# Splitting the attention weights and building the 4-bit weights in pieces beside the MLP units

## What is computed

```python
x = x + layernorm(mamba_mixer_and_mlp(layernorm(x)))      # L0_attn: mixer, then a gated MLP of width 1792
x = x + layernorm(lora_mlp(layernorm(x)))                 # L0_ffn: gated MLP of width 1376, LoRA of rank 16
x = x + layernorm(attention(layernorm(x)))                # L1_attn: 32 heads of 16, 8 kv heads, causal, RoPE
x = x + layernorm(lut_linear(layernorm(x)))               # L1_ffn, below
# lut_linear, with e = norm of a token's row:
w_l = dequant_kbit(qweight, lut4, 4)    # (512, 512): each weight is one of 16 values of its row
w_h = dequant_kbit(qweight, lut8, 8)    # the same from 256 values
y = where(e > 64, x @ w_h.T, x @ w_l.T) + bias
```

## Time and profile before

| | us |
|---|---|
| median of 3 runs | 1904.93 (1902.29 to 1907.94) |
| the profiled execution | 1906.81 |
| its span, first to last instruction | 1905.0 |
| TensorE busy | 1666.1 (87%) |
| VectorE busy | 1037.7 (54%) |
| ScalarE busy | 793.0 (42%) |
| GpSimd busy | 601.3 (32%) |

### The profile page before, as it was taken

The page is one execution under the profiler, slowest core; times in us unless marked ns, Lnnn a source line. Parts: engine busy times, 40 slices in busy tenths (PEclk is TensorE's granted clock), DMA queues, the critical chain, the costliest instruction groups (busy, mean ns, idle before and its releaser), DMA issues. The chain is left out here.

```text
span 1905.0 us, 25873 instructions
## 1 busy us (share of the span) xinstructions
PE 1666.1 (87%) x8965; PEld 1393.2 (73%) x8965; DVE 1037.7 (54%) x2013; ACT 793.0 (42%) x1603; POOL 601.3 (32%) x792
## 2 busy tenths in 40 slices
PE   5999986999999999999999998028889889899884
PEld 4899874888888888778778887026778778777763
DVE  7888755522232226753433234755767767767772
ACT  4676643222122112212212111406867776776760
POOL 5454551211111113431111134124344444444422
PEclk9999997999999999999999999558999999999996
DMA  4000002000011012310110001200000000000000
GB/s 134 13 23 12 1 1 78 23 23 21 25 34 31 23 35 75 103 59 15 34 37 27 21 23 44 76 1 1 1 1 12 12 1 12 12 1 13 12 7 18
DMA packets 28548, 52.16 MB, mean 27 GB/s; under 512 B 3520, under 2 KB 4704, under 8 KB 28416
## 3 DMA queue, kind: packets, MB, share of 16 engines
q1 hardware_dynamic: 28416, 50.47, 8.5%
HBM read 42.07 MB, written 8.39 MB: 26 GB/s over the span
## 5 line engine op out<-in xcount | busy, mean ns | idle before, releaser
L1171 POOL TENSOR_TENSOR m_a_lo<-m_prod,m_a_hi 128x512 fp32r<-128x512 f32 x100 | 130.8, 1308 | 640.3 <-ACT m_a_hi L1229 640.2
L1345 DVE TENSOR_TENSOR m_prod<-m_prod,m_ps 128x512 f32<-128x512 f32 x100 | 68.8, 688 | 482.0 <-ACT m_prod L1225 481.9
L114 PE MATMUL m_ps<-m_hT_hi,m_w_hi 128*128 128x512 f32 x800 | 317.8, 397 | 7.5 <-DVE m_w_lo L1327 5.3
L116 PE MATMUL m_ps<-m_hT_hi,m_w_lo 128*128 128x512 f32 x800 | 317.7, 397 | 0.0
L115 PE MATMUL m_ps<-m_hT_lo,m_w_hi 128*128 128x512 f32 x800 | 317.1, 396 | 0.0
L1225 ACT ACTIVATE m_prod<-m_ps 128x512 f32<-128x512 f32 x100 | 59.7, 597 | 577.9 <-PE m_ps L116 577.9
L1802 ACT ACTIVATE t_p<-t_ps,t_nmax 128x128 f32<-128x128 f32 (+1 forms) x512 | 181.0, 424 | 75.0 <-DVE t_nmax L1924 74.8
L1924 DVE TENSOR_REDUCE t_nmax<-t_ps 128x2 f32<-128x512 f32 (+1 forms) x192 | 132.0, 688 | 96.6 <-PE t_ps L1993 60.1
L114 PEld LDWEIGHTS m_ps<-m_hT_hi,m_w_hi 128*128 128x128 f32 x800 | 151.3, 189 | 44.1 <-issue 5.7
L115 PEld LDWEIGHTS m_ps<-m_hT_lo,m_w_hi 128*128 128x128 f32 x800 | 151.2, 189 | 36.3
L116 PEld LDWEIGHTS m_ps<-m_hT_hi,m_w_lo 128*128 128x128 f32 x800 | 151.0, 189 | 36.4
(11 more groups left out here) (259 smaller groups left out, 3732.4 us busy)
## 6 DMA issues: line engine op xcount, KB each, us to landing
m_raw<-in_w_mlp SPq DMA_DIRECT2D x75, 256.0 KB, 2.7
a_xt<-in_x SPq DMA_DIRECT2D x8, 512.0 KB, 3.8
m_old<-in_x SPq DMA_DIRECT2D x16, 256.0 KB, 4.2
x_store<-stream SPq DMA_DIRECT2D x4, 1024.0 KB, 5.1
m_old<-x_store SPq DMA_DIRECT2D x16, 256.0 KB, 2.7
out<-t_yl SPq DMA_DIRECT2D x16, 256.0 KB, 2.0
q_raw<-in_w_attn SPq DMA_DIRECT2D x10, 256.0 KB, 5.1
a_att<-in_w_mixer SPq DMA_DIRECT2D x8, 256.0 KB, 2.8
```

The lines of the kernel that those rows point to most:

```text
L114: pe.matmul(out, w_hi, x_hi, start=first, stop=False)
L116: return pe.matmul(out, w_lo, x_hi, start=False, stop=last)
L1171: pool.tensor_tensor(a_lo[:, n % 2, :], prod[:, :], f(a_hi[:, n % 2, :]), ALU.subtract).then_inc(lo, 1)
L1345: dve.tensor_tensor(prod[:, :], prod[:, :], ps[:, U + TURN_AT["unit", n, 0] % 2, :], ALU.mult).then_inc(prodd, 1)
```

## The change

`split_weights` and `lut_weights_by_tree` are gone. Their work is done inside `mlps`, and attention follows directly.

- The tree is cut into 16 pieces of 128 columns (`TREE_COLS`), one for every two spots of groups 1, 2 and 3 (`TREE_AT`). At the first of the two ScalarE fills eight leaves and VectorE makes four masks; at the second VectorE does the 15 predicated copies. Leaves lie in `m_tok` and planes, tables and masks in `m_old`, which those groups don't use. SyncE stores each piece to a DRAM buffer `w4_store` (`store_tree`).
- In the last group ten pieces "attn" load and split the attention weights into the weight set that is free then, and four pieces "lut" load the 4-bit weights back, turn them on TensorE and split them. The table `LATE` says which at which spot.
- Buffers are shared so that this fits: block 0's `hT` lies in the LUT weights, `ln2` in `bias`, the mixer's `hT` too in the LUT weights.
- In attention GpSimd clears `v` and `kT` behind the first two `roots("x", ...)`; those who read them wait for it themselves.
- `JOBS_AT` is another table, and with it some steps of VectorE and GpSimd are at other slots.

```diff
+TREE_COLS, TREE_BITS = 128, 4
+TREE_LEAVES = 2 ** TREE_BITS // 2
+TREE_PIECES = DT * DIM // TREE_COLS
+TREE_SPOTS = [(g, i, j) for g in (1, 2, 3) for i in range(NB) for j in range(GROUPS[g][1])]
+TREE_AT = {TREE_SPOTS[2 * r + part]: (r, part) for r in range(TREE_PIECES) for part in range(2)}
+LATE = ((("attn", 0), ("attn", 1)), (("attn", 2), ("attn", 3)), (("attn", 4), ("attn", 5)), (("lut", 0),), (("attn", 6),),
+        (("lut", 1),), (("attn", 7),), (("lut", 2),), (("attn", 8), ("attn", 9)), (("lut", 3),))
...
+            def tree_leaves(r):
+                act.wait_ge(tree_in, 48)
+                if r:
+                    act.wait_ge(picks, TREE_PICKS * r)
+                else:
+                    act.wait_ge(tp, TPB * NB)
+                for n in (*range(1, TREE_LEAVES), 0):
+                    if n == 0 and r:
+                        act.wait_ge(tree_out, 16 * r)
+                    act.activation(leaf(n), entry(r, 2 * n), ACT.Copy).then_inc(leaves, 1)
...
+            def store_tree(r):
+                sp.wait_ge(picks, TREE_PICKS * (r + 1))
+                sp.dma_start(w4_store[:, r * TREE_COLS:(r + 1) * TREE_COLS], leaf(0)).then_inc(tree_out, 16)
...
+            def tree_picks(r):
+                dve.wait_ge(masks, TREE_BITS * (r + 1))
+                dve.wait_ge(leaves, TREE_LEAVES * (r + 1))
+                for n in range(TREE_LEAVES):
+                    dve.copy_predicated(leaf(n), mask(0), entry(r, 2 * n + 1)).then_inc(picks, 1)
...
+                    for n in range(0, TREE_LEAVES, 2 * step):
+                        dve.copy_predicated(leaf(n), mask(p), leaf(n + step)).then_inc(picks, 1)
...
+            def lut_turned(q):
+                pe.wait_ge(raw_in[q % RAW], 16 * (q // RAW + 1))
+                k = turn_free(("lut", q, 0))
+                for a in range(DT):
+                    mm = pe.transpose(ps[:, G + k, a * P:(a + 1) * P], raw[:, q % RAW, a * P:(a + 1) * P], ident)
...
 JOBS_AT = (
-    (("k", 1, 1, 0), ("q", 3, 0, 0)),
+    (("q", 3, 0, 0),),
...
+    (("x", 0, 1, 1), ("k", 1, 1, 0)),
     (("kv", 0, 0, 1),),
-    (("x", 0, 1, 1),),
...
-    (("back", 1, 0, 0), ("l", 0, 0, -1)),
-    (("l", 1, 0, -1), ("q", 2, 1, 1)),
-    (("back", 1, 1, 0), ("h", 0, 1, -1)),
+    (("back", 1, 0, 0), ("h", 0, 1, -1)),
+    (("q", 2, 1, 1), ("l", 0, 0, -1)),
+    (("back", 1, 1, 0), ("l", 1, 0, -1)),
...
-                if n == 6 and in_batch(b + 1):
+                if n == 7 and in_batch(b + 1):
                     rope_sum(0, b + 1)
...
-                if n in (0, 5) and in_batch(b + 1):
-                    normalise("x", n // 5, b + 1)
+                if n in (0, 4) and in_batch(b + 1):
+                    normalise("x", n // 4, b + 1)
...
-                if n in (17, 20) and in_batch(b - 1):
-                    normalise("h", n // 20, b - 1)
+                if n in (17, 18) and in_batch(b - 1):
+                    normalise("h", n - 17, b - 1)
```

More of the change, by code:

```diff
@@ L116, in product @@
     return pe.matmul(out, w_lo, x_hi, start=False, stop=last)
[L119 to L152, removed]
 PAIRS, CONVS = 5, 3
@@ L997, in weight_pieces @@
             pieces.append(piece)
+    spots = [(NG - 1, i, j) for i in range(NB) for j in range(GROUPS[NG - 1][1])]
+    for spot, beside in zip(spots, LATE):
+        for what, k in beside:
+            of_weight[what, k, 0] = len(pieces)
+            ready.setdefault(spot, []).append(len(pieces))
+            pieces.append((what, k, 0))
     return pieces, of_weight, ready
@@ L1026, with mlps @@
 LORAS = [q for q, piece in enumerate(PIECES) if piece[0] == "lora"]
-def mlps(nc, d, consts, stream, x1_store):
+LUTS = [q for q, piece in enumerate(PIECES) if piece[0] == "lut"]
+def mlps(nc, d, consts, stream, x1_store, w4_store, lut, bias, late, late_2):
     with ExitStack() as ctx:
         m = Memory(nc, ctx)
-        sets = [[m.sb(f"m_w{s}_{p}", [P, 3 * UNIT], F32R) for p in ("hi", "lo")] for s in range(2)]
+        late_cols = late.rearrange("p k n -> p (k n)")
+        sets = [[m.sb(f"m_w0_{p}", [P, 3 * UNIT], F32R)[:, :] for p in ("hi", "lo")],
+                [late_cols[:, 0:3 * UNIT], late_cols[:, 3 * UNIT:6 * UNIT]]]
         RAW = 3
@@ L1046, in mlps @@
         f_rs, e_rs = (m.sb(f"m_{n}_rs", [P, 4, TPB]) for n in "fe")
-        hT_hi = m.sb("m_hT_hi", [P, DT, TOK], F32R)
-        hT_lo = m.sb("m_hT_lo", [P, DT, TOK], F32R)
+        hT_hi, hT_lo = ([own] + [m.sb(f"m_hT{i}_{p}", [P, DT, BT], F32R) for i in range(1, NB)] for own, p in zip(lut, ("hi", "lo")))
         ps = m.banks("m_ps")
@@ L1063, in mlps @@
         stored, const = sem("stored"), sem("const")
+        tree_in, leaves, masks, picks, tree_out, lut_tp, bias_in = (
+            sem(n) for n in ("tree_in", "leaves", "masks", "picks", "tree_out", "lut_tp", "bias_in"))
         x_in, x1_out = (ap.rearrange("(t p) n -> p t n", p=P) for ap in (d["x"], x1_store))
@@ L1083, in units_to, with leaf, mask, entry @@
             return NB * GROUPS[g][0]
+        def leaf(n):
+            return tok[:, n // 4, n % 4 * TREE_COLS:(n % 4 + 1) * TREE_COLS]
+        def mask(p):
+            half, at = p // 2, 256 + p % 2 * TREE_COLS
+            return old[:, half, at:at + TREE_COLS].bitcast(I32)
+        def entry(r, k):
+            return entries[:, r * TREE_COLS // DIM, k:k + 1].broadcast_to([P, TREE_COLS])
+        def late_low(k):
+            return late[:, 10 + k, :] if k < 8 else late_2[:, k - 8, :]
         @block.sync
@@ L1199, in piece_high @@
                        .then_inc(w_high, 1)
+                elif kind == "attn":
+                    act.wait_ge(down, units_to(NG - 1))
+                    act.activation(late[:, u, :], raw[:, q % RAW, :], ACT.Copy, scale=0.25 if u < 4 else 1.0).then_inc(w_high, 1)
+                elif kind == "lut":
+                    act.wait_ge(lut_tp, u + 1)
+                    act.wait_ge(gate_up, unit_at(NG - 1, 0, GROUPS[NG - 1][1] - 1) + 1)
+                    act.activation(lut[0][:, u, :], ps[:, G + TURN_AT["lut", q, 0] % 2, :], ACT.Copy).then_inc(w_high, 1)
                 else:
@@ L1420, in gate_and_up @@
                         col = slice(j * UNIT + at + a * P, j * UNIT + at + (a + 1) * P)
-                        mm = product(pe, ps[:, bank, :], w_hi[:, col], w_lo[:, col], hT_hi[:, a, cols], hT_lo[:, a, cols],
+                        mm = product(pe, ps[:, bank, :], w_hi[:, col], w_lo[:, col], hT_hi[i][:, a, :], hT_lo[i][:, a, :],
                                      a == 0, a == DT - 1)
@@ L2077, in project @@
                 pe.wait_ge(tl, h + 1)
-                weights = (l_hi, l_lo) if what == "l" else (w_hi, w_lo)
+                hi, lo = (l_hi, l_lo) if what == "l" else (w_hi, w_lo)
                 ks_ = range(DT) if what == "kv" else range(2 * part, 2 * part + 2)
```

196 lines of the change are left out of this document (101 added, 95 removed), and 4 rows, old and new, of the table JOBS_AT.

## The result

| | before | after |
|---|---|---|
| median, us | 1903.61 (4 runs, 1900.17 to 1907.94) | 1828.99 (4 runs, 1826.81 to 1830.80) |
| the profiled execution | 1906.81 | 1826.81 |
| its span | 1905.0 | 1825.0 |

What follows compares the result with a forecast made beforehand. It took the block between MLPs and attention to lie wholly on the path, with no engine full in attention's full batches. -62.2 - 7.2 - 2.4 + 3.9 - 9.1 - 3.8 = -80.8 gave 1825 us, range 1808 to 1841.

Steps and rivals of the forecast that it cites:

- The block between: Between MLP stage and attention: the weight-splitting and tree block goes and attention starts where it did, -62.2 us.
- the clearing: Start of attention: GpSimd clears buffers behind the first roots, so the first normalisation comes 7.2 us earlier; cover 1 us.
- First tiles: First tiles of attention: reordered pieces shorten an hT_lo wait and start GpSimd's stacks earlier, 1.2 us each, -2.4 us.
- The MLP stage: MLP stage: tree pieces hidden beside the matmuls; TensorE pays 2.4 for transposes and 1.5 for a late load, +3.9 us.
- Full batches: Seven full batches of attention: the new table saves 1.3 us a batch, -9.1 us in sum.
- Step (a): Slot 2 of a full batch: k (1, 1) moves to slot 5, leaving one wait for GpSimd's stacks, -0.5 us.
- (c): Products h and l in a full batch: both h first, hT_lo waits go from 2.1 to 1.4, -0.7 us.
- The end: Last batch of attention: both h first, the second l follows without a gap, so the bias starts earlier, -3.8 us.
- A: Rival for attention's table: it brings the named waits to nothing, -28 us for -9.1, 1806 us; chance 0.10.
- B: Rival for attention's table: it costs 1.0 us a batch, with kT waits growing, 1841 us; chance 0.15.
- D: Rival for MLP groups 1 to 3: VectorE becomes the bound if masks and copies cost 2.36 each, 2342 us; chance 0.01.
- E: Rival at the MLP stage's end: late pieces hold it or attention back, half of the 62 stays, 1856 us; chance 0.02.

Runs made afterwards that it cites:

- the old table: The changed kernel with the table of attention pieces, and its VectorE and GpSimd steps, as before the change: 1842.62 us, ratio 0.9666.
- slots 0 to 16 alone: The changed kernel with only these slots of the new attention table, later slots as before the change: 1837.99 us, ratio 0.9642.
- slots 17 to 23 alone: The changed kernel with only these slots of the new attention table, earlier slots as before the change: 1830.31 us, ratio 0.9607.
- the kernels with more copies: The changed kernel with 16 or 40 more predicated copies in each tree piece: 1827.49 us (ratio 0.9594) and 1872.54 us (ratio 0.9817).
- the kernel with 150: The changed kernel with 150 identity transposes on TensorE behind the last down projection: 1829.12 us, ratio 0.9609.

## Why the prediction was right, and where it wasn't

1. **The block between** and **the clearing** were right to 0.1 us. Their price could be read off the timeline as distances between two rows, with no duration to be assumed. The cover of the clearing was larger than I said (2.8, not 1), since in the new table x of tile 1 goes ahead of kv: ScalarE's copy of v comes 11.9 us behind the normalisation, and 10.3 with the old table. The clearing ends at 9.0. I had taken the copy's place from the order of before, though the same change moves it. That -62.1 and -7.1 are whole gains rests on the distances in the two traces; only the second was also taken back by an experiment.
2. **First tiles**: -3.2 for -2.4. With the old table this stretch takes 31.7 again, so it is the table's, and with slots 0 to 16 alone 28.7, so it is theirs. The 30.3 of slots 17 to 23 alone is for the most part not the table's work: its half clock ends sooner, and the first q is done 7.5 behind the normalisation in place of 8.7.
3. **The MLP stage** is the mis-sized term, +6.1 for +3.9, and my sign that it ends within 5 us of 1199.7 did not come true. The four sets of transposes (0.45 each, 1.8 for my 2.4), the cover on VectorE and the late second load were right. The wait of 2.1 lies between my bounds of 1 and 4; the load landed 3.5 behind its issue, not 2.7. Transposes and late unit make 5.8; the other 0.3 lies ahead of the first unit. What I left out is what a wait does in a stretch at full clock: about 1.6 us more at 1.2 GHz. I had asked what the wait takes from TensorE, and not what TensorE does after it. In the four profiles in which the clock held, the stage takes 4.0 to 4.3 more than before from its first product to its last, close to my 3.9.
4. **Full batches**: -7.6 for -9.1, with the last batch. Step (a) was right on the stacks (1.0 to 0.4), but I took every later wait as it was. The one for the kT copies in slot 15 grows by 0.3, and of 0.6 for slots 0 to 16 come 0.2. In (c) the waits behind both h are 0.5 + 0.5, not 0.8 + 0.6: -1.1, of which a `pT_lo` wait takes 0.2, so -0.95 for -0.7.
5. **The end**: -6.1 for -3.8. From l to the last bias it is -4.3, near the 3.8 that I worked out with the second l at full clock. Another 1.6 lies ahead of the first l, from the last maximum on, where I had looked for nothing. It goes with the clock: that stretch has 12.6 us at half clock before and 9.8 after. In the ten other kernels with the same end the whole end takes 52.5 to 54.5 us, so -6.1 is near the large side of what this term does (-4.2 to -6.3), and that is luck.
6. **Rivals.** A (all waits go) is out: 2.4 of the 3.4 us for `hT_lo` stay. B (the table costs 1.0 a batch) is out: it gives 1.1, though a kT wait does grow. C (all four loads late) is out: one load was late. D is out by the cost of a copy, 0.30, and by the kernels with more copies: TensorE pays only when VectorE is more than some 4.8 us late. E is out: VectorE starts 1.03 behind the last addition.

## What to carry to other kernels

A wait on the engine that bounds a dense stretch may cost twice: its own length, and a stretch at the lower clock behind it; look at the granted clock of the window after each wait. In a ring of two buffers a job waits for the reader of the job two before it, so when an order is changed, write down for each job whose reader it now waits for: it need not be the one whose data it needs. And when work is hidden, measure how much more would fit: the cover here took 16 more copies a piece for nothing and failed at 40.

## What the runs showed of the hardware

- Predicated copies of 128 columns take 0.30 us each in the trace and 0.215 from start to start. One that starts while GpSimd's operation on 128x512 runs takes up to 1.43 and ends with it; this was so in all twelve pieces where the two met. The sums out of PSUM that start inside the same operation (`stream<-m_ps,stream`, 19 of them) keep their 0.69.
- A wait of 1.8 to 2.3 us on TensorE, in otherwise unbroken work, was followed by a stretch at half clock in six of ten profiles (waits of 1.84 to 2.33); four (1.77 to 1.79) kept the full clock.
- 150 transposes of 128 columns in a row, and nothing else, kept the granted clock at full for 16 us. The Trainium skill ("TensorE: Matmul & The Clock Gate", section "Part 4: PE-mode transpose") has it that transposes don't engage the full rate; the windows from 1190 to 1205 of the kernel with 150, at 1.00, say otherwise for a clock that is full when they start. Whether they also raise it from half, no run here shows:

```profile
1195.00:1200.00 5.00, 5.00 (x49) 5.00 (x48) 3.53 (x9) 0.00 (x0) 3.69 (x4) 1.00 0.00 0
```
